# Output stage of a long-convolution and FFN kernel: dense copies of V for the transposes, a low half computed on GpSimd, stores on ScalarE's queue, and the last down-projections ahead of the transposes

## What is computed

```python
xn = layernorm(x)
proj = xn @ in_proj_w + in_proj_b            # v, ctrl0, ctrl1: 256 channels each
v = proj[..., :256]
for i in range(2):
    h = implicit_filter(2048, ...)           # a small MLP over time, one filter a channel
    v = fft_conv(v, h)                       # causal convolution over the 2048 positions
    v = v * gated_control(ctrl[i], ...)      # short convolution, then x * sigmoid(x @ gw + gb)
attn = v @ out_proj_w + out_proj_b
hh = bitlinear(xn, w_fc) + gate * (xn @ v_.T @ fast_b.T @ u.T)
ffn = bitlinear(relu(hh) ** 2, w_proj)       # ternary weights with a scale
out = x + attn + ffn
```

## Time and profile before

| | us |
|---|---|
| median of three runs | 912.26 (908.46, 912.26, 917.91) |
| the profiled execution | 918.76 |
| its span in the trace | 917.1 |
| TensorE busy | 849.1 (93%) |
| VectorE busy | 624.8 (68%) |
| ScalarE busy | 472.5 (52%) |
| GpSimd busy | 248.0 (27%) |
| mean DMA rate | 155 GB/s |

### The profile page before, as it was taken

One profiled execution on the slowest core, in us unless ns is written; L12 is line 12 of the kernel. 1 busy time (PEld: TensorE's weight loads), 2 busy tenths in 40 slices (PEclk: granted clock), 3 DMA queues, 4 the chain that ended last, 5 costly groups with the idle time before them and its releaser, 6 DMA issues.

```text
span 917.1 us, 25923 instructions
## 1 busy us (share of the span) xinstructions
PE 849.1 (93%) x9916; PEld 706.6 (77%) x9917; DVE 624.8 (68%) x1036; ACT 472.5 (52%) x692; POOL 248.0 (27%) x260
## 2 busy tenths in 40 slices
PE   6768999999999996999999999998999998999995
PEld 2357888888888865878888888786877887788995
DVE  8735889889889883555555565565546565666884
ACT  4934777777787763534444444443434444443221
POOL 2523466466465402011111111211012101200111
PEclk8978999999999997999999999999999999999998
DMA  7542432432432338677877978677768886962893
GB/s 209 186 178 70 145 132 92 153 121 92 158 116 93 132 80 268 130 171 165 179 154 159 192 157 189 136 171 163 173 124 177 179 155 124 201 109 67 235 335 121
DMA packets 84382, 142.02 MB, mean 155 GB/s; under 512 B 12829, under 2 KB 62382, under 8 KB 83310
## 3 DMA queue, kind: packets, MB, share of 16 engines
q1 hardware_dynamic: 71214, 101.65, 47.2%
q0 software_dynamic: 10032, 36.44, 12.2%
q10 hardware_dynamic: 3088, 3.30, 1.1%
HBM read 97.39 MB, written 43.97 MB: 154 GB/s over the span
## 4 chain that ended last, share of the span: by engine, by line
PE 42%; DMA 10%; DVE 5%; issue 3%; ACT 1%; SPq 1%; DVEq 0%; POOL 0%; ACTq 0%
PE py L1300 12%; PE pp L1281 11%; DMA lead<-filters 9%; PE pf L1250 9%; PE pf L1256 2%; PE py L1337 2%; PE py L1268 2%; DVE r L1090 1%; PE pp L447 1%; PE pp L449 1%; PE pp L448 1%; DVE pp L1080 1%; DVE xb L1085 1%; DVE r_lo L1095 1%; SPq L1435 1%
## 5 line engine op out<-in xcount | busy, mean ns | idle before, releaser
L1300 PEld LDWEIGHTS py<-vwin,lead 64*64 64x64 f32 x5120 | 137.1, 136 | 37.7 <-issue 37.7
L1300 PE MATMUL py<-vwin,lead 64*64 64x128 f32 (+4 forms) x5120 | 151.1, 269 | 12.5 <-DMA lead<-filters 11.5
L1196 ACT ACTIVATE r_hi<-r 128x512 fp32r<-128x512 f32 x128 | 80.8, 631 | 153.2 <-DVE r L1090 153.2
L1191 ACT ACTIVATE r<-pf,fscale 128x512 f32<-128x512 f32 x128 | 87.9, 687 | 117.5 <-PE pf L1256 117.4
L1281 PE MATMUL pp<-wproj,r_hi 128*128 128x256 f32 x512 | 135.4, 297 | 8.8 <-DVE r_lo L1095 2.9
L1095 DVE TENSOR_TENSOR r_lo<-r,r_hi 128x512 fp32r<-128x512 f32 x128 | 95.3, 745 | 67.1 <-ACT r_hi L1196 67.0
L1250 PE MATMUL pf<-tokens,split_a 128*128 (+1 forms) x512 | 139.4, 393 | 0.0
L1281 PE MATMUL pp<-wproj,r_lo 128*128 128x256 f32 x512 | 127.0, 281 | 0.0
L1281 PEld LDWEIGHTS pp<-wproj,r_hi 128*128 128x128 f32 x512 | 96.6, 189 | 24.4 <-issue 9.5
L488 POOL TENSOR_SCALAR lead<-lead,norms 128x256 f32<-128x256 f32 x64 | 113.7, 1789 | 3.4 <-POOL norms L482 3.4
L646 DVE SCALAR_TENSOR_TENSOR xc<-ctrl,taps,xc 128x512 f32<-128x512 f32 x128 | 97.0, 777 | 18.9 <-ACT xc L720 18.2
(11 more groups left out here) (183 smaller groups left out, 1548.2 us busy)
## 6 DMA issues: line engine op xcount, KB each, us to landing
lead<-filters SPq DMA_DIRECT2D x128, 320.0 KB, 6.3
xnT_hbm<-split_b SPq DMA_DIRECT2D x32, 512.0 KB, 3.2
tokens<-xnT_hbm POOLq DMA_DIRECT2D x30, 512.0 KB, 7.7
lead<-in_attn_x SPq DMA_DIRECT2D x16, 512.0 KB, 3.9
gc_hbm<-xc SPq DMA_DIRECT2D x16, 512.0 KB, 2.7
GC<-gc_hbm SPq DMA_DIRECT2D x32, 256.0 KB, 6.9
out<-GC POOLq DMA_DIRECT2D x16, 512.0 KB, 6.1
GC<-in_attn_x POOLq DMA_DIRECT2D x9, 512.0 KB, 12.0
```

The lines of the kernel that those rows point to most:

```text
L1191: act.activation(r[j][:, :], pf[:, j, :], ACT.Relu, scale=fscale[:, m:m + 1]).then_inc(relu_done, 1)
L1196: act.activation(r_hi[j][:, :], r[j][:, :], ACT.Copy).then_inc(r_hi_done, 1)
L1300: last = pe.matmul(py[g % 2][q * BW:(q + 1) * BW, side, l, :, A:NB], tile[rows, q * PAIR + l, j * BW:(j + 1) * BW], vwin[g % 2][rows, q, l ...
```

## The change

Four edits in the output stage:

- ScalarE copies the 8 blocks of V of each tile into a dense buffer `ys[p % 2]` (laid over `Tmid` and over `vwin`), and the transposes read that. `Tmid` and `vwin` become one tensor each for this. T(p) waits for `ys_ready`, copy p+2 waits until T(p) has read the buffer.
- The low half of tiles 2 to 15 is computed by GpSimd. VectorE waits for it before `gated(p)` (that of p-2), since `gated(p)` overwrites `yg`.
- The stores are issued by ScalarE, store p-2 behind the high half of p and the copy of p+2. ScalarE also waits for the last ones to land.
- TensorE does both last down-projections before T(0), and VectorE does `low(15, 7)` before `gated(0)`.

```diff
--- before.py
+++ after.py
@@ -870,8 +870,11 @@
         wproj = sb("wproj", [P, HT, D], F32R)
         vrank = sb("vrank", [P, KT, PARTS, RANK], F32R)
         lowmask = sb("lowmask", [HALF, 1])
-        Tmid = [sb(f"Tmid{i}", [P, SIDES * PAIR, MID * BW]) for i in range(2)]
-        vwin = [sb(f"vwin{i}", [P, SIDES, PAIR, B, NB]) for i in range(2)]
+        Tmids = sb("Tmid", [P, 2, SIDES * PAIR, MID * BW])
+        vwins = sb("vwin", [P, 2, SIDES, PAIR, B, NB])
+        Tmid, vwin = [Tmids[:, i] for i in range(2)], [vwins[:, i] for i in range(2)]
+        ys = [Tmids[:, :, :, :].rearrange("p i c j -> p (i c j)").rearrange("p (t s) -> p t s", t=TB),
+              vwins[:, :, :, :, :, :].rearrange("p i b l n a -> p (i b l n a)").rearrange("p (t s) -> p t s", t=TB)]
         srow = sb("srow", [P, D])
         xb = sb("xb", [P, TT, D])
         bo_row = sb("bo_row", [P, D])
@@ -906,7 +909,7 @@
         wo = xb[:, 0:KT, :]
         out_tiles = out.rearrange("n (q i p) d -> (n q) p i d", i=TT, p=P)
         wo_hi_ready, wo_split = sem("wo_hi_ready"), sem("wo_split")
-        yT_mm, yg_ready = sem("yT_mm"), sem("yg_ready")
+        yT_mm, yg_ready, ys_ready = sem("yT_mm"), sem("yg_ready"), sem("ys_ready")
         yg_hi_done, yg_split = sem("yg_hi_done"), sem("yg_split")
         out_mm, out_ready = sem("out_mm"), sem("out_ready")
         out_saved = [sem(f"out_saved{i}") for i in range(KEPT)]
@@ -1054,11 +1057,9 @@
                     load_xb(c, kept=True)
             load_xb(NCH - 1, kept=True)
 
-            for p in range(NCH):
-                pool.wait_ge(out_ready, p + 3)
-                pool.dma_start(out_tiles[position(p)], sums[p % KEPT]).then_inc(out_saved[p % KEPT], 16)
-            for j in range(KEPT):
-                pool.wait_ge(out_saved[j], 16 * ((NCH - 1 - j) // KEPT + 1))
+            for p in range(2, NCH):
+                pool.wait_ge(yg_hi_done, p + 1)
+                pool.tensor_tensor(ygs[p % 2][1], yg[p % 2], ygs[p % 2][0].bitcast(F32), ALU.subtract).then_inc(yg_split, 1)
 
         @block.vector
         def _(dve):
@@ -1150,17 +1151,17 @@
 
             for order in range(ORDERS):
                 lagging(dve, order, lambda m, it, first: body(order, m, it, first), True)
+            low(NCH - 1, HT - 1)
             gated(0)
-            low(NCH - 1, HT - 1)
             yg_low(0)
             gated(1)
             scale(NCH - 1)
             add(NCH - 1, sums[KEPT - 1])
             yg_low(1)
             for p in range(2, NCH):
+                dve.wait_ge(yg_split, p - 1)
                 gated(p)
                 summed(p - 2)
-                yg_low(p)
             for p in (NCH - 2, NCH - 1):
                 summed(p)
 
@@ -1175,7 +1176,7 @@
                 act.wait_ge(group_mm, G + 1)
                 if order:
                     act.wait_ge(y_out, G - GROUPS // ORDERS + 3)
-                act.activation(vwin[g % 2][:, :, :, :, :].rearrange("p b l n a -> p b l (n a)"),
+                act.activation(vwin[g % 2].rearrange("p b l n a -> p b l (n a)"),
                                Vs[:, :, bass.ds(channels(m, g), PAIR), :], ACT.Copy).then_inc(window_done, 1)
 
             act.wait_ge(mask_ready, 1)
@@ -1222,12 +1223,30 @@
                 act.wait_ge(out_mm, c + 1)
                 act.activation(ygs[i][0], yg[i], ACT.Copy).then_inc(yg_hi_done, 1)
 
+            def copy(p):
+                c = position(p)
+                if p >= 2:
+                    act.wait_ge(yT_mm, p - 1)
+                act.activation(ys[p % 2].rearrange("p t s -> p s t"), V[:, :, c // CPB, (c % CPB) * TB:(c % CPB) * TB + TB], ACT.Copy).then_inc(ys_ready, 1)
+
+            def store(p):
+                act.wait_ge(out_ready, p + 3)
+                act.dma_start(out_tiles[position(p)], sums[p % KEPT]).then_inc(out_saved[p % KEPT], 16)
+
+            act.wait_ge(y_out, GROUPS + 2)
+            copy(0)
+            copy(1)
             act.wait_ge(fc_mm, NCH * HT + HT)
-            high(0, 0)
-            high(1, 1)
-            with act.Fori(1, NCH // 2) as m:
-                for i in range(2):
-                    high(m * 2 + i, i)
+            for p in range(NCH):
+                high(p, p % 2)
+                if p + 2 < NCH:
+                    copy(p + 2)
+                if p >= 2:
+                    store(p - 2)
+            for p in (NCH - 2, NCH - 1):
+                store(p)
+            for j in range(KEPT):
+                act.wait_ge(out_saved[j], 16 * ((NCH - 1 - j) // KEPT + 1))
 
         @block.tensor
         def _(pe):
@@ -1331,10 +1350,11 @@
                 lagging(pe, order, body)
 
             def transposed(p):
-                i, c = p % 2, position(p)
+                i = p % 2
+                pe.wait_ge(ys_ready, p + 1)
                 pe.wait_ge(yg_ready, p + 1)
                 for t in range(TB):
-                    last = pe.transpose(pT[i][:, t, :, :].rearrange("p k j -> p (k j)"), V[:, :, c // CPB, (c % CPB) * TB + t], ident[:, :])
+                    last = pe.transpose(pT[i][:, t, :, :].rearrange("p k j -> p (k j)"), ys[i][:, t, :], ident[:, :])
                 last.then_inc(yT_mm, 1)
 
             def projected(p):
@@ -1352,10 +1372,10 @@
                 for order in range(ORDERS):
                     mixed(order, far)
                 pe.wait_ge(y_out, GROUPS + 2)
+                proj(NCH - 1, HT - 2)
+                proj(NCH - 1, HT - 1)
                 transposed(0)
-                proj(NCH - 1, HT - 2)
                 transposed(1)
-                proj(NCH - 1, HT - 1)
                 pe.wait_ge(wo_split, 1)
                 pe.wait_ge(relu_done, NCH * HT + 2)
                 projected(0)
```

## The result

The changed kernel takes 921.38 us in the median of six runs, the kernel before, run beside it, 913.12. The ratio is 1.010 with a 95% interval of 1.0068 to 1.0132, so + 9 us (6 to 12). It is slower by about the 1% that a measurement can tell. The forecast was 918.0 in a range of 911 to 924.

The account below looks back on a forecast made before the run. Output stage bound equally by TensorE's work and a two-tile ring through VectorE and ScalarE, 4.06 us per tile. Start + 3.6, ring + 6.3, store - 0.9, close - 3.3 give + 5.7 on the median 912.26: 918.0 us, range 911 to 924.

Parts of the forecast that it names:

- The two limits: Output stage before: TensorE's own work and a ring over two tiles through VectorE and ScalarE, both 4.06 us per tile.
- The ring with GpSimd: Output stage after: low half on GpSimd at 2.39 us makes the ring 4.51 per tile against TensorE's 3.75; + 6.3 us.
- T to P: From the start of a tile's eight transposes to its own 24 output matmuls: 5.16 us before, 6.05 forecast after.
- The copies: ScalarE's copy per tile, taken as 1.03 us and hidden; upper end twice that, moving only the first two copies, 0.4 us.
- The start: Reordered beginning of the output stage: low half 1 and tile 1's output matmuls come 3.62 us later; + 3.6 us.
- The clock: Rival: TensorE's idle time at the stage's start lowers its granted clock, + 1 to + 3 us, 919 to 921; chance 0.23.
- The end: From the last sum's end to the span's end: 8.4 us becomes 4.2, through store (- 0.9) and close (- 3.3).
- The close: Time after the last transfer: 4.1 us becomes 0.8 as GpSimd finishes earlier, - 3.3; rival that it stays 4.1, chance 0.12.
- The store: Last store, issued by ScalarE, lands 3.2 us after its issue, the median of the hardware queue's 512 KB stores; - 0.9 us.
- the late VectorE queue: At the start, VectorE's operations queued behind tile 0's delayed low half all shift, putting low half 1 3.62 us later.
- within 1%: Outcome between 1% faster (903.1 us) and 1% slower (921.4 us) than the kernel before; chance 0.75.
- the other side: Rival, output stage: the ring doesn't carry GpSimd's time, so not slower: 910.3 us, or 907.4 with TensorE's 3.75; chance 0.07.

Follow-up runs that it names:

- high_twice: The kernel before, with ScalarE's rounding of yg done twice in a row in each output-stage tile: ratio 1.0109, + 10.0 us.
- combined: The kernel before, with stores issued by ScalarE and dense copies for the transposes from tile 2 on; start and low halves unchanged: ratio 0.994, - 5.5 us.
- halves_strided: The kernel before, with stores on ScalarE and gate product, high and low halves each in two halves of 256 rows, no copies: ratio 0.9969, - 2.8 us.
- start_only: The kernel before, with only the start reordered (last down-projections before the first transposes, last low half of r before the first gate product): ratio 1.0038, + 3.5 us.
- after_filled: The changed kernel, with 20 matmuls that compute nothing placed in TensorE's wait before tile 0's output matmuls: ratio 1.0062, + 5.7 us against the kernel before.
- after_low_dve: The changed kernel, with the low halves of tiles 2 to 15 back on VectorE: ratio 0.9981, - 1.7 us against the kernel before.

## Why the prediction was right, and where it was off

**The two limits.** Confirmed: high_twice and combined for the ring, halves_strided for TensorE's part. They stood less level than the prediction had it: its 5.16 held some 0.15 of slack, so TensorE was the nearer limit by about 0.07 per tile.

**The ring with GpSimd.** T to P was put at 6.05 and is 5.95, two tiles at 9.01 and are 8.92; 14 steps at + 6.3 and are + 5.9. GpSimd's 2.39 came from two rows of the same form in another stage, and the 14 rows here have 2.37 and 2.40. No lengthening by VectorE's work appeared, as was argued from PSUM operands and the order in time; the page's rule on exclusion (the Trainium skill, SBUF — State Buffer, "SBUF: two separate sides") was neither contradicted nor tested.

**The copies.** The term was mis-sized: 1.03 taken, 2.01 to 2.06 measured, the upper end that was kept for the range.

```profile
L1230 ACT ACTIVATE vwin<-V 128x1024 f32<-128x1024 f32 x8 | 16.5, 2061 | 0.0
```

The nearest row had its steps on the reading side in PSUM, these write with steps of 512 bytes in SBUF. The Trainium skill (SBUF — State Buffer, "Door 1: The DMA port swizzle"), which speaks of a penalty for each access that crosses into another line of 16 bytes, was the better guide, and the trace agrees in direction: 2.0 against 1.03. The sum hardly moved, since ScalarE with 1.06 + 2.0 + 0.4 stays under 3.75 and only the first two copies are waited for: T(0) is 0.16 later than forecast, T(1) waited 0.69, and low half 1 is 0.18 later.

**The start.** 3.62 forecast for low half 1, 3.80 in the changed kernel, 3.92 in start_only.

**The clock.** The forecast named it as a rival with a chance of 0.23, + 1 to + 3. It came: 2.0 us in this trace by after_filled, 0.5 to 1 us in the traces of after_low_dve and start_only. Its 2.0 are the main part of the difference between the likeliest value, + 5.7, and the trace's + 8.4; the end adds 1.0 and the start's copies 0.2, and the ring takes 0.4 back. The idle time was counted about rightly (from 842 to 846 alone TensorE was busy 2.17 of 4), and the trace of before had such a case; the chance was set too low.

**The end.** 8.41 became 5.17, forecast 4.2. The close is short, as forecast, though its reason was put only half rightly: GpSimd's DRAIN is not gone, it runs earlier. The store was the mis-sized term: its transfers run past 921.0, over 3.6 us behind an issue at about 917.4, and the 16 stores have a median of 4.9, not the 3.2 taken from the stores of an earlier stage. The page of before had a nearer row, the same stores with a median of 6.1:

```profile
out<-GC POOLq DMA_DIRECT2D x16, 512.0 KB, 6.1
```

The forecast was thus right in sign and in mechanism: the ring through GpSimd and the late VectorE queue are the two main terms, and the start within 0.2 us (3.62 forecast, 3.80 measured), the ring within 0.4. The total, 918.0 in a range that holds 921.4, was low by the clock and the landing of the last store. By its chances the forecast stood on "within 1%", and the measured ratio is 1.010, on the line. The lower end of its range, 911, is called the middle of the other side, whose two values are 910.3 and 907.4; it lies above both.

## What to carry to other kernels

When a busy engine shows no wait, add up the chain from one of its operations through the other engines back to it and divide by the number of buffers; if that equals the engine's own work, both must be shortened, and an engine that "has time" has none if it lies in that chain. Move work to a slower engine only out of the chain, or after the chain has been cut, for example by handing over half tiles. A reordered start is to be priced by the queue that stands behind the delayed operation and by the clock that an idle TensorE loses, not by TensorE's wait.

## What the runs showed of the hardware

- A ScalarE copy of 128x1024 f32 that writes SBUF with steps of 512 bytes takes 2.0 us; with such steps on the PSUM side it takes 1.03.
- Eight transposes whose weight loads read with steps of 512 bytes hold TensorE 1.10 us, dense ones 0.79; one such load takes 256 ns instead of 140. TensorE's own work per tile was 3.75 instead of 4.06.
- Where TensorE waited 2.1 us behind two waits of 0.7 to 0.9, the granted clock fell to 0.5 for the matmuls that followed: 24 of them took 5.26 us in one trace and 4.21 in another with the same waits, instead of 2.96. Twenty matmuls that compute nothing, placed in the wait, kept it at 1.00; P(1) came 0.5 to 2 us sooner.
- GpSimd's program ended with a DRAIN of 3.17 us (behind its wait for the stores) or 7.0 us (from its last operation's start); ScalarE's, behind its wait for the stores, took 0.01. With GpSimd closing behind the stores the span ended 4.1 us behind the last transfer, with ScalarE waiting for them about 1 us; from the last sum to the end that was 3.6 us less.
- GpSimd's subtraction of 128x1024 f32 took 2.36 to 2.40 us, VectorE's 1.23; of 128x512, 1.31 and 0.69.
